# A layernorm, linear-recurrence and mixture-of-experts layer on 8 cores: the prologue rebuilt and the tail reordered

## The reference, cut to what matters

```python
x = L0_attn_x                                # (2, 8192, 1024) f32; 16384 rows, 2048 per core
xn = layernorm(x)                            # no scale, no shift, eps 1e-5
# recurrent branch
a = sigmoid(A_diag)                          # 64 states
u = xn @ B                                   # (rows, 64)
h[t] = a * h[t-1] + u[t]
s = h @ C + xn @ D
# expert branch
logits = sigmoid(xn @ gate_w + gate_b)       # 16 experts, the best 2 per row
v, idx = top_k(logits, 2);  v = v / sum(v)
mlp(x, wg, wu, wd) = (silu(x @ wg) * (x @ wu)) @ wd          # 1024 -> 512 -> 1024
g = silu(xn + mlp(xn, shared) + sum_k v[k] * mlp(xn, experts[idx[k]]))
out = x + s * g
```

## Time and profile before

| | |
|---|---|
| Time of three runs | median 740.28 us (739.29 to 740.67) |
| The profiled execution's own time | 733.69 us |
| Its span on core 6 | 732.1 us |
| bn_stats of 512 columns (L280, L281) | 0.69 and 0.68 us; bn_aggr (L283) 0.21 |
| Norm of a tile, GpSimd (L314) / ScalarE (L317) | 1.20 / 1.23 us |
| Eviction of 8 transposes, ScalarE (L340) | 1.02 us |
| Silu and product of a shared group (L392, L399) | 0.60 and 0.69 us |
| One recurrence block: 8 matmuls (L466), scan (L475) | 1.89 and 1.27 us |
| One-hot matrices, VectorE: L590, L594, L596, L599 | 2.29 x 2, 1.49, 0.55, 1.48 us |
| Tail: L1077, L1093 VectorE; L1091 ScalarE; L1095 GpSimd | 1.22, 1.22; 1.06; 2.36 us (median) |
| One ACT_TABLE_LOAD | 1.28 us, 5 in the program (L415, L392 twice, L527, L1053) |

### The profile page before, as it was taken

The page is one execution under the profiler, slowest core; times in us unless marked ns, Lnnn a source line. Parts: engine busy times, 40 slices in busy tenths (PEclk is TensorE's granted clock), DMA queues, the critical chain, the costliest instruction groups (busy, mean ns, idle before and its releaser), DMA issues.

```text
span 731.9 us, 7940 instructions; the slowest of 8 cores (721.0 to 732.1 us)
## 1 busy us (share of the span) xinstructions
PE 454.5 (62%) x2742; PEld 246.0 (34%) x2776; DVE 245.6 (34%) x437; ACT 176.1 (24%) x242; POOL 163.6 (22%) x167
## 2 busy tenths in 40 slices
PE   0126649965995484782872975838838787874530
PEld 0123324433552252450540543515514333331210
DVE  3763533472211121120210211201202567772235
ACT  0233321301322131320320321313203132221111
POOL 2110110022332132141230331412202123231113
PEclk9999968999999698797896997988979899997785
DMA  8971129401999999999999999999997565663421
GB/s 191 235 249 58 45 100 159 87 27 56 154 179 198 186 213 173 194 199 199 183 194 203 189 164 204 199 190 165 197 207 213 191 220 197 217 213 124 169 109 57
DMA packets 29705, 122.71 MB, mean 168 GB/s; under 512 B 5277, under 2 KB 5661, under 8 KB 22880
## 3 DMA queue, kind: packets, MB, share of 16 engines
q0 software_dynamic: 17136, 81.15, 58.7%
q1 hardware_dynamic: 12528, 41.03, 16.3%
HBM read 150.87 MB, written 33.55 MB: 252 GB/s over the span
## 4 chain that ended last, share of the span: by engine, by line
DMA 33%; PE 31%; DVE 14%; ACT 7%; issue 6%; DVEq 4%; POOL 2%; POOLq 1%; SPq 0%; ACTq 0%
DMA y_dram<-ysb,pidx 25%; PE ps L764 10%; PE ps L378 8%; PE ps L382 8%; DVEq L79 4%; DVE xgT L1085 4%; DVE xgT L1088 3%; DMA x_sb<-x_in 2%; ACT ysb L1091 2%; ACT xgT L1053 2%; DMA xn_dram<-xgT 2%; DMA a_t<-adiag 2%; PE ps L722 1%; POOL ysb L1095 1%; PE ps L466 1%
## 5 line engine op out<-in xcount | busy, mean ns | idle before, releaser
L764 PE MATMUL ps<-ring,xgT 128*128 128x512 bf16 (+1 forms) x368 | 101.0, 414 | 115.2 <-ACT ysb L775 89.3
L777 DVE COPY ysb<-ps 128x512 f32<-128x512 f32 (+1 forms) x48 | 33.1, 691 | 206.5 <-DMA y_dram<-ysb,pidx 120.9
L764 PEld LDWEIGHTS ps<-ring,xgT 128*128 128x128 bf16 (+1 forms) x384 | 36.7, 109 | 174.7 <-issue 152.0
L378 PE MATMUL ps<-xgT,ring 128*128 128x320 bf16 x512 | 82.2, 304 | 8.4 <-ACT silu L392 7.0
L382 PE MATMUL ps<-xgT,ring 128*128 128x320 bf16 x512 | 80.3, 300 | 0.0
L775 ACT ACTIVATE ysb<-ps 128x512 f32<-128x512 f32 (+1 forms) x48 | 28.6, 595 | 206.4 <-DMA y_dram<-ysb,pidx 135.2
L392 ACT ACTIVATE silu<-ps 128x320 f32<-128x320 f32 (+1 forms) x80 | 37.6, 470 | 136.2 <-PE ps L382 135.9
L399 DVE TENSOR_TENSOR xgT<-silu,ps 128x320 bf16<-128x320 f32 x64 | 31.2, 488 | 115.2 <-ACT silu L392 115.2
L1069 PE MATMUL ps<-ring,xnT 128*128 128x512 bf16 x252 | 67.2, 412 | 2.1 <-DVE ysb L1093 1.9
L1095 POOL TENSOR_TENSOR ysb<-ysb,x_sb 128x1024 f32<-128x1024 f32 x16 | 38.7, 2417 | 125.0 <-DVE ysb L1093 125.0
L378 PEld LDWEIGHTS ps<-xgT,ring 128*128 128x128 bf16 x512 | 48.5, 99 | 32.7 <-issue 14.5
(11 more groups left out here) (130 smaller groups left out, 471.1 us busy)
## 6 DMA issues: line engine op xcount, KB each, us to landing
ring<-ewg POOLq DMA_DIRECT2D x16, 1024.0 KB
ring<-ewu POOLq DMA_DIRECT2D x16, 1024.0 KB, 24.9
ring<-ewd POOLq DMA_DIRECT2D x16, 1024.0 KB, 23.6
ring<-y_dram SPq DMA_DIRECT2D x32, 512.0 KB, 5.4
x_sb<-x_in SPq DMA_DIRECT2D x16, 512.0 KB, 25.7
out<-ysb SPq DMA_DIRECT2D x16, 512.0 KB, 3.0
xn_dram<-xgT SPq DMA_DIRECT2D x16, 256.0 KB, 3.2
ysb<-x_in SPq DMA_DIRECT2D x6, 512.0 KB, 7.4
```

What stands on the lines that cost most here:

```text
L378: PE.op(lambda e, c=c: e.matmul(bank(p)[:, 0:n], slot_gu(m, c, ic), rhs(c), start=(c == 0), stop=(c == 7)))
L764: f = lambda q, k=k, h=h, dst=dst: q.matmul(dst, inter(e, k, o, n), slot_d(m, k, h), start=(k == 0), stop=(k == 3))
L777: k2 = V.sig(lambda q, to=to, src=src: q.tensor_copy(to, src))
```

## The change

**Prologue.** All 18 tiles of x get places: the halo tiles in ring place 5, the last four in `ysb`. Ten loads are issued at the start (`LEAD`), the rest one per tile behind `xn_store`, with no other wait. `xnb` has 8 buffers: five in `xg`, whose memset is gone. The 1/sqrt goes to ScalarE as Ln and Exp; GpSimd does every norm, as (x - mean) * rstd. The eviction of a tile's transposes is appended two tiles later than before, behind the next pair's Ln and Exp. The loads of the shared gate and up weights are issued behind the norm of the 13th tile; those of ring places 2 to 5 right after the last norm.

```diff
+            A.op(lambda e: e.activation(lnt[:, t:t + 2], var, AF.Ln, bias=cst(C_EPS, 1)))
+            A.drain()
+            return A.sig(lambda e: e.activation(rstd[:, t:t + 2], lnt[:, t:t + 2], AF.Exp, scale=-0.5))
...
+            T_XN[t] = G.sig(lambda e: e.tensor_scalar(
+                buf, x_buf(t), mv[:, 2 * t:2 * t + 1], rstd[:, t:t + 1], ALU.subtract, ALU.mult))
...
         for i in range(len(ORDER) + AHEAD):
...
+            if 2 <= i < len(ORDER) + 2:
+                ln_evict(ORDER[i - 2], i - 2)
+            if i < len(ORDER):
                 ln_norm(t, i, t_stats[t])
                 ln_transpose(t, i)
-                ln_evict(t, i)
                 xn_store(t, i)
+                if i + LEAD < len(ORDER):
+                    load_x(ORDER[i + LEAD])
+                if i == 12:
+                    load_w(0)
+                    load_w(1)
```

```diff
+            T_UPC[g] = A.sig(lambda e: e.activation(upc[p], bank(2 + p), AF.Copy))
+            FREE_U[p] = T_UPC[g]
         def sh_mul(g):
...
+            G.wait(T_UPC[g])
+            T_MUL[("s", g)] = SIL_USED[p] = G.sig(lambda e: e.tensor_tensor(
+                dst, silu[:, p * 512:p * 512 + 512], upc[p], ALU.mult))
...
+        until("cnt")
+        sh_gu(0)
+        sh_mul(0)
+        sh_gu(1)
+        sh_gu(2)
+        until("E")
+        sh_mul(1)
+        sh_mul(2)
+        for g in range(3, 5):
+            sh_gu(g)
+            sh_mul(g)
+        until("inv")
+        until("idx")
...
         for j in range(5):
             gather(j)
+        T_HALO = recur(-1)
+        for g in range(5, 16):
+            sh_gu(g)
+            sh_mul(g)
+            if g in (6, 8, 10, 12):
+                recur((g - 6) // 2)
+        A.wait(R["V"])
+        R["ex"] = A.sig(lambda e: e.activation(sm(2), sm(0), AF.Exp, scale=-1.0))
+        st_w()
...
+        A.wait(*[T_MUL[("s", g)] for g in (14, 15)])
         for j in expert_tiles(0):
             transpose_tile(0, j)
             gather(j + 5)
```

```diff
+            if e == E - 1:
+                PE.wait(FREE_G[0], FREE_G[1], FREE_U[0], FREE_U[1], prev_scan[0],
+                        T_W[M_SD], T_W[M_D0], T_W[M_D1], *[T_MUL[("s", g)] for g in range(16)])
+                A.wait(R["nmr"], FREE_XGT[e])
+                tail_front(0)
+                tail_sum(0)
             PE.wait(T_W[m + 2], *[T_MUL[(e, ic)] for ic in range(4)])
...
             T_S[t] = A.sig(lambda e: e.activation(g, a, AF.Silu))
+            if t + 1 < NT:
+                tail_sum(t + 1)
             V.wait(T_S[t], T_P2[t])
             T_H[t] = V.sig(lambda e: e.tensor_tensor(g, g, bank(b + 2, 2), ALU.mult))
             G.wait(T_H[t])
             T_F[t] = G.sig(lambda e: e.tensor_tensor(g, g, x_fin(t), ALU.add))
             SP.wait(T_F[t])
             T_O[t] = SP.dma(lambda e: e.dma_start(out=out[t * 128:(t + 1) * 128, :], in_=g), s_o[t % 3])
+            if t + NXR < NT:
+                T_XR[t + NXR] = SP.dma(lambda e: e.dma_start(out=x_fin(t + NXR), in_=x_rows(t + NXR)), s_xr[t])
```

More of the change, by code:

```diff
@@ L196, in build_nc @@
         s_x = [semaphore(f"s_x{t}") for t in range(NT + 2)]
-        s_st = [semaphore(f"s_st{i}") for i in range(3)]
+        s_st = [semaphore(f"s_st{i}") for i in range(NXB)]
         s_r = [semaphore(f"s_r{i}") for i in range(NRING)]
@@ L238, in w_src, with m_of @@
                 return (swg, swu)[m]
[L239 to L245, removed]
+            if m >= M_SD and m < M_SD + 3:
+                return (swd, dmat[0], dmat[1])[m - M_SD]
+            e, j = divmod(m - 2, 3) if m < M_SD else (E - 1, m - M_SD - 3)
+            return (ewg, ewu, ewd)[j][e]
+        M_SD = 2 + 3 * (E - 1)
+        def m_of(e):
+            return 2 + 3 * e if e < E - 1 else M_SD + 3
         T_W = {}
@@ L291, in ln_stats @@
[L291 to L301, removed]
@@ L694, in gather @@
             if j == 0:
-                G.wait(R["idx"], T_Z, *[(s, s.n) for s in s_st])
+                G.wait(R["idx"], *[(s, s.n) for s in s_st])
             if j >= NXG:
@@ L729, in transpose_tile @@
             if e == 0 and j == 0:
-                A.wait(T_HALO, R["val"], R["tot"], R["U"], T_TR[NT - 1])
-                A.wait(*[(s, s.n) for s in s_st])
+                A.wait(T_HALO, R["val"], R["U"], R["V"])
             if p == 2:
@@ new lines, in tail_front @@
+        def tail_front(t):
+            b = 4 * (t % 2)
+            A.wait(T_XR.get(t), T_S.get(t - 2))
+            T_AN[t] = A.sig(lambda e: e.activation(ab[t % 2], x_fin(t), AF.Identity,
+                                                   bias=nmr[:, t:t + 1], scale=rstd[:, t:t + 1]))
+            PE.wait(T_A1.get(t - 2))
+            for h in range(2):
+                for k in range(4):
+                    f = lambda e, h=h, k=k: e.matmul(bank(b + h), interS[:, k * T_OWN + t * 128:k * T_OWN + (t + 1) * 128],
+                                                     slot_d(M_SD, k, h), start=(k == 0), stop=(k == 3))
+                    if (h, k) == (1, 3):
+                        T_P1[t] = PE.sig(f)
+                    else:
+                        PE.op(f)
+            PE.wait(T_H.get(t - 2))
+            for h in range(2):
+                PE.op(lambda e, h=h: e.matmul(bank(b + 2 + h), hs[:, HALO + t * 128:HALO + (t + 1) * 128],
+                                              csb[:, h * 512:(h + 1) * 512], start=True, stop=False))
+                for c in range(8):
+                    f = lambda e, h=h, c=c: e.matmul(
+                        bank(b + 2 + h), xnT[:, c * T_OWN + t * 128:c * T_OWN + (t + 1) * 128],
+                        slot_d(M_D0 if c < 4 else M_D1, c % 4, h), start=False, stop=(c == 7))
+                    if (h, c) == (1, 7):
+                        T_P2[t] = PE.sig(f)
+                    else:
+                        PE.op(f)
@@ L1099, in build_nc @@
         for t in range(2):
             T_YF[t] = y_load(t)
-        tail_front(0)
+        PE.wait(T_DV, T_DA)
         for t in range(NT):
```

310 lines of the change are left out of this document (125 added, 185 removed).

## The result

The changed kernel takes 716.63 us (four runs, 716.0 to 721.14) against 739.78 for the kernel before on the same chip: ratio 0.9726, 95% interval 0.9688 to 0.9765, so 23 us faster. The forecast was 681 with 650 to 704 around it: the direction was right, the time lies above the range.

What follows compares the result with a forecast made beforehand. Bounds: a chain between engines late in the prologue, DMA queues in the experts, waits for x in the tail. 732.1 - 40 + 17 - 36.6 = 672.5; 1.6 around it and the 6.6 median offset gave 681 us, range 650 to 704.

Steps and rivals of the forecast that it cites:

- Prologue: Start of the kernel up to expert 0: last logits at 56 us, expert 0 at 142 instead of 182, -40 us.
- Nothing waits for a buffer: Prologue: normalized-row stores land in 3.4 us, and each of 8 buffers is reused only after some 16, so no wait.
- Shared groups and router: Between last logits and expert 0: groups start at 66, list matmuls end at 88, expert 0 starts at 142 us.
- Expert 15: Last expert: later gate and up weights plus the early front delay its down products to 572 or 573, +17 us.
- Tail: Final tiles: early x loads and the reordered sum give 7.25 us a tile, 114 instead of 150.6, -36.6 us.
- Offset: Whole kernel: the profiled execution lay 6.6 us below the median of the runs, so 6.6 us was added.
- Tables: Rival, prologue: Ln and Exp evict each other's ScalarE tables, 12 us lost, 693 us; chance 0.07.
- No exclusion: Rival, tail: GpSimd's addition does not hold up VectorE as forecast, 6.1 us a tile, 664 us; chance 0.10.
- Expert 15 in time: Rival, last expert: its weights arrive in time and only the front costs, +6, 670 us; chance 0.16.
- Half a prologue: Rival, prologue: DMA traffic and GpSimd work holding up ScalarE put expert 0 at 162, 701 us; chance 0.11.
- A slower expert stage: Rival, experts: cores in step disturb each other's transfers, the 363 us grow, at 160 GB/s 754 us total; chance 0.05.

Runs made afterwards that it cites:

- Experiment 1: The kernel before, with each of its nine GpSimd norms in another form of one or two operations; 734.75 us in its one run.
- experiment 2: The changed kernel with the norm as (x * rstd) + nmr, nmr formed on VectorE for each pair; 696.58 us, ratio 0.9517.
- experiment 12: Changed kernel: multiply-add norm, weights after stores, r_U and addition on VectorE, old ring order and front, later shared weights, four early shared groups; 649.42 us, ratio 0.8744.
- Experiment 5: The changed kernel with the old ring order and the first front behind expert 15's down products again; 690.64 us, ratio 0.9454.
- experiment 6: The changed kernel with its new ring order, but the first front moved back behind expert 15's down products; 711.11 us, ratio 0.9631.
- experiment 9: The changed kernel with x for tiles 12 to 15 loaded as late as in the kernel before; 738.01 us, ratio 1.0007.

## Why the forecast was wrong, step by step

**Prologue, -40 forecast, -5.9 measured (the step that failed).** The step is the sentence "GpSimd's 1.20 and ScalarE's 1.02 a tile ... lie beside that", and "two norms 2.5" behind the last tile. 1.20 was read from a norm of the form (x*r)+n, and the diff has (x-mean)*r. I looked up the engine, the operation and the shape, and took the two ALU operations as free. Eighteen norms of 3.77 in place of 1.20 make GpSimd the bound: 30 us later at the last logits. Experiment 1 shows the price with nothing else changed, experiment 2 puts the logits back at 55.

**Nothing waits for a buffer (false as well, hidden).** 3.4 us to landing was the median of 16 stores, most of them issued after 48 us, where the DMA share is 0.23; the first three in the trace of before, issued at 33 to 41 us at a DMA share of 0.9 to 1.0, took 14.4, 11.6 and 9.0, and the median hid them. Beside loads of x and weights the median is 21.6 us, and once the norms are fast ScalarE waits 20.97 for it (experiment 2); with the stores cleared first, expert 0 comes at 138 in place of 162 (experiment 12, `r_U` and one shared group included). With the norm's price right this step would still have been wrong: experiment 2's 0.9517 of 739.78 is 704, the upper end of the range.

**Shared groups and router: about right by luck.** From the last logits to the end of the list matmuls 29 us passed (86.3 to 115.4) where the forecast had 32. But I counted five groups ahead of the list; the code makes the list matmuls in the same step as `E`'s products, behind three. Two more groups stand after it, so the rest took 60.8 us and not 54. `r_U` was put at 4.5 and took 7.9, and TensorE waited 6.59 for it.

**Expert 15, +17 forecast, +25 measured (mis-sized).** The mechanism was right: waits for `ewg` and `ewu`, the front ahead of the down products. Against expert 0, the last weights land 6 us later than in the earlier trace rows (555.35 - 176.15 = 379.2 against 373), and the front with its start took 9 us (565.9 to 574.83) in place of 6.5; that is the 8. Experiment 5 gives the whole back; experiment 6 parts it roughly.

**Tail, -36.6 forecast, -36.9 measured (right).** The rows L869 3.21, L878 3.44 and the period 7.13 to 7.19 are as forecast, 7.25 a tile; the last tile of the earlier trace rows was the right row to build on. That GpSimd and VectorE share SBUF interfaces with contention for two-input instructions, as the Trainium skill has it (GPSIMD Engine Reference, table of specifications), the traces bear out: 3.21 with GpSimd's addition beside it, 1.28 without. How the gain divides was only partly right: 0.35 to 0.4 a tile for the reorder where I had 0.17, and 20 us for the early x in this order. Of the 150.6 us the new order alone, with x late, leaves 135.3 (experiment 9), and both together 113.8.

**Offset.** The forecast added 6.6 us, as the profiled execution of before was that far under the median. That of after is 0.6 under its own. The terms miss by 34.1 + 8.1 - 0.3 = 41.9, less the 6.0 of the offset 35.9; measured less forecast is 716.6 - 681 = 35.6.

**The rivals.** Tables: refuted, one load at 12.40. The Trainium skill's rule (ScalarE: Activation LUTs, the section on table sets), one set for both functions, holds here. No exclusion: refuted by 3.21 and 3.44. Expert 15 in time: refuted by its two waits. Half a prologue (expert 0 at 162): nearest in size, but expert 0 came at 176 and not 162, and DMA and ScalarE, which it blamed, were not the cause. A slower expert stage: refuted, the share is 1.01 at 190 GB/s and experiment 5 has 374.0 us for it. The range failed because no rival priced a GpSimd norm above 1.20: the unknown was taken for a known.

## What to carry to other kernels

A duration belongs to one form of an instruction: before it is carried over, compare the operations in it, not just engine, name and shape, and if no row has the new form, bound it as an unknown. When a slow step is made fast, ask at once which transfer it was spacing out: here the stores behind it were late as soon as the norms were cheap. A median to landing holds for the traffic in which most of the transfers ran; look at the ones that ran in the traffic to come. An engine that is full can still gain by taking work over, if the other engine's instruction holds it up for longer than that work takes itself.

## What the runs showed of the hardware

GpSimd's `tensor_scalar` of 128 x 1024, f32 to bf16, takes 1.19 us for two operations out of multiplication and addition, 2.84 for one alone (a multiplication or a subtraction) and 3.79 for a pair with a subtraction (experiment 1). That one operation costs more than two was the larger surprise; (x*r)*r is cheaper than x*r. Whether a neutral second operation would speed up a lone one, as in `r_U`, was not run.

A 256 KB store lands 2.6 to 3.4 us after issue by the medians of the kernels after and before. Where loads of x alone fill the DMA engines (share 1.0) it takes 10.5 to 13.5 us (experiments 2 and 12), and with six 1 MB casting weight loads beside it, issued by another queue, 39 to 46 (experiment 2). So here the time at which the bulk loads were issued decided how long a small transfer took.

The exclusion in the tail picks its side: where GpSimd's addition starts just behind L866, L869 and the addition stretch (3.21 and 3.44); where L866 starts later, for want of y rows, it is stretched itself (2.10 to 2.56) and the addition keeps its 2.35. In the first case VectorE loses 1.9 us a tile, in the second 0.8 to 1.3, besides its wait for the y rows.
